# Making a scatter wait for the previous unit's scatter of the same tile, and no longer for TensorE's products

## The reference

```
x  = L0_attn_x                       # 16 x 512 tokens, 256 features, float32
xn = layernorm(x)
out = x + attention(xn) + ffn(xn)

attention: Q, K = elu(xn W + b) + 1;  V = xn Wv + bv
           KV = K^T V per sequence;  (Q KV / (Q . sum K)) Wo^T + bo     # linear attention
ffn:       scores = sigmoid(xn gate^T)                                  # 16 experts
           keep 2 of 4 groups, then the top 4 experts, weights scaled to 2.5
           sum over the 4 experts of weight * (silu(xn up_e) down_e)    # 256 -> 128 -> 256
           + silu(xn shared_up) shared_down
```

## Time and profile before

| | |
|---|---|
| timed runs, median of 3 | 972.14 us (971.48 to 979.37) |
| the profiled execution: time | 966.78 us |
| its span, first to last instruction | 964.8 us |
| mean granted clock of TensorE | 0.929 of full speed |
| TensorE, VectorE, ScalarE, GpSimd busy | 80%, 73%, 57%, 60% of the span |
| expert stage, first sum scatter to output copy | 485.8 to 929.97 us |

### The profile page before, as it was taken

The page is one execution under the profiler, slowest core; times in us unless marked ns, Lnnn a source line. Parts: engine busy times, 40 slices in busy tenths (PEclk is TensorE's granted clock), DMA queues, the critical chain, the costliest instruction groups (busy, mean ns, idle before and its releaser), DMA issues. The chain is left out here.

```text
span 964.8 us, 19765 instructions
## 1 busy us (share of the span) xinstructions
PE 768.8 (80%) x5264; PEld 704.2 (73%) x5264; DVE 700.7 (73%) x2390; ACT 553.1 (57%) x1142; POOL 581.4 (60%) x581
## 2 busy tenths in 40 slices
PE   4999999999999999997377767687676776776760
PEld 4899999999899988886266666676675775765750
DVE  5989898888888999999466555665556665656550
ACT  5677677676677766663155545554545544555440
POOL 1067766666777766666556565665555566656662
PEclk9999999999999999999599899998889888999795
DMA  5245554554445433332599888888887887888889
GB/s 156 71 171 193 186 176 179 194 187 175 149 159 188 146 129 129 114 116 112 177 288 284 239 266 266 252 261 268 245 252 250 270 267 247 265 264 261 249 277 304
DMA packets 142316, 202.15 MB, mean 210 GB/s; under 512 B 16176, under 2 KB 117184, under 8 KB 142208
## 3 DMA queue, kind: packets, MB, share of 16 engines
q1 hardware_dynamic: 114144, 116.47, 41.8%
q0 software_dynamic: 28064, 84.43, 22.8%
HBM read 104.19 MB, written 105.04 MB: 217 GB/s over the span
## 5 line engine op out<-in xcount | busy, mean ns | idle before, releaser
L574 POOL DMA_INDIRECT rows_by_expert<-xn,f_id x286 | 279.8, 978 | 194.4 <-issue 64.5
L490 POOL DMA_INDIRECT rows_by_expert<-xn,slots_now x192 | 196.9, 1026 | 122.8 <-PE bank_a L316 59.1
L1245 DVE TENSOR_TENSOR xt_l<-bank_a,xt_h 128x512 fp32r<-128x512 f32 x143 | 98.3, 687 | 97.1 <-ACT xt_h L698 67.4
L719 ACT ACTIVATE hid<-bank_x 128x256 f32<-128x256 f32 x143 | 55.3, 387 | 147.3 <-PE bank_x L316 71.5
L698 ACT CAST xt_h<-bank_a 128x512 fp32r<-128x512 f32 x143 | 83.8, 586 | 77.7 <-PE bank_a L1446 49.7
L316 PE MATMUL bank_y<-we,hs_h 128*128 x284 | 68.0, 333 | 68.4 <-DVE hs_l L1268 45.3
L316 PE MATMUL bank_a<-we,hs_h 128*128 x288 | 70.0, 337 | 61.9 <-DVE hs_l L1268 42.5
L316 PEld LDWEIGHTS bank_y<-we,hs_h 128*128 128x128 f32 x284 | 49.4, 210 | 82.3 <-issue 82.2
L316 PEld LDWEIGHTS bank_a<-we,hs_h 128*128 128x128 f32 x288 | 51.4, 216 | 75.0 <-issue 74.6
L316 PE MATMUL bank_y<-ws,hs_h 128*128 128x256 f32 x512 | 94.4, 282 | 1.4 <-DVE hs_l L997 1.4
L316 PE MATMUL bank_x<-xt_h,ws 128*128 128x512 f32 x256 | 92.1, 401 | 0.0
(11 more groups left out here) (289 smaller groups left out, 2427.7 us busy)
## 6 DMA issues: line engine op xcount, KB each, us to landing
xn<-rows_by_expert SPq DMA_DIRECT2D x215, 272.0 KB
x_in<-rows_by_expert SPq DMA_DIRECT2D x71, 272.0 KB
rows_by_expert<-spare SPq DMA_DIRECT2D x22, 544.0 KB
x_in<-in_L_attn_x_dram SPq DMA_DIRECT2D x16, 512.0 KB
out_dram<-rows_by_expert SPq DMA_DIRECT2D x8, 1024.0 KB
rows_by_expert<-xn,f_id POOLq DMA_INDIRECT x286
rows_by_expert<-xn,slots_now POOLq DMA_INDIRECT x256
w_raw<-in_L_ffn_expert_up_dram SPq DMA_DIRECT2D x32, 64.0 KB
```

Source lines behind the costliest of these rows:

```text
L490: G.indirect_dma_start(out=half_rows[:, :], in_=xn[:, c % NB, s, 0:RW], in_offset=None, out_offset=bass.IndirectOffsetOnAxis(ap=slots_now[ ...
L574: G.indirect_dma_start(out=half_rows[:, :], in_=f_y[u % YB][:, tile], in_offset=None, out_offset=bass.IndirectOffsetOnAxis(ap=f_id[:, u % ...
L719: S_.activation(f_hid[u % 2], X[u % 2][:, 0:UR], ACT.Silu).then_inc(fs_done, 1)
L1245: V.tensor_tensor(f_l[u % 4], A[u % 2][:, :].rearrange("p (c s t) -> p c s t", c=KD, s=2), f_h[u % 4].bitcast(F32), ALU.subtract).then_inc ...
```

## The change

The waits on `fd_done` and `fu_done` go. Tile 0 of unit u now waits until tile 0 of unit u - 1 has landed, and tile 1 until tile 1 of unit u - 1 has. So that such a landing can be told apart, there is a semaphore for each tile, and two classes of units in place of four: four semaphores as before, each counting 16 a unit. SP's waits follow: for each of the two classes both tiles' semaphores are waited for, with one number from the table.

```diff
-    CLS = 4
+    CLS = 2
...
-        added = [sem(f"added{i}") for i in range(CLS)]
+        added = [[sem(f"added{k}_{tile}") for tile in range(2)] for k in range(CLS)]
...
         def adds_until(u):
-            return PRIMED + 32 * (u // CLS + 1)
+            return PRIMED + 16 * (u // CLS + 1)
...
+            def landed(u):
+                for k in range(CLS):
+                    needed = four_from(mybir.EngineType.SP, 2 + k, u, PRIMED, PRIMED + 16 * UNITS)
+                    for tile in range(2):
+                        sp.wait_ge(added[k][tile], needed)
+                        sp.sem_inc(sums_free, 1)
+
             def load_sums(u):
                 if u == 4:
                     sp.wait_ge(scattered[(B - 1) % NB], scatters_until(B - 1))
                 if u >= YB:
-                    sp.wait_ge(added[(u - YB) % CLS], adds_until(u - YB))
-                for k in range(CLS):
-                    sp.wait_ge(added[k], four_from(mybir.EngineType.SP, 2 + k, u, PRIMED, PRIMED + 32 * UNITS))
-                    sp.sem_inc(sums_free, 1)
+                    for tile in range(2):
+                        sp.wait_ge(added[(u - YB) % CLS][tile], adds_until(u - YB))
+                landed(u)
...
             for u in range(UNITS):
                 pool.wait_ge(y_ready, u + 1)
                 pool.wait_ge(id_ready, u + 1)
-                pool.wait_ge(added[u % CLS], adds_until(u - CLS) if u >= CLS else PRIMED)
                 for tile in range(2):
-                    if u >= 2:
-                        if tile == 0:
-                            pool.wait_ge(fd_done, min(u + 2, UNITS))
-                        else:
-                            pool.wait_ge(fu_done, min(u + 4, UNITS))
+                    if u == 0:
+                        pool.wait_ge(added[0][tile], PRIMED)
+                        pool.wait_ge(added[1][tile], PRIMED)
+                    if u >= 1:
+                        pool.wait_ge(added[(u - 1) % CLS][tile], adds_until(u - 1))
                     G.indirect_dma_start(
                         out=half_rows[:, :], in_=f_y[u % YB][:, tile], in_offset=None,
                         out_offset=bass.IndirectOffsetOnAxis(ap=f_id[:, u % YB, tile:tile + 1], axis=0)
-                    ).then_inc(added[u % CLS], 16)
+                    ).then_inc(added[u % CLS][tile], 16)
```

More of the change, by code:

```diff
@@ L410, in _ @@
             sp.wait_ge(scattered[(B - 3) % NB], scatters_until(B - 3))
-            sp.wait_ge(scattered[(B - 2) % NB], scatters_until(B - 2) - 16 * CLS)
+            sp.wait_ge(scattered[(B - 2) % NB], scatters_until(B - 2) - 16 * SUB)
             for k in range(CLS):
-                sp.wait_ge(added[k], PRIMED)
+                for tile in range(2):
+                    sp.wait_ge(added[k][tile], PRIMED)
             row_of = {}
@@ L442, in _ @@
                     load_sums(u - (ROWS_AHEAD - SUMS_AHEAD))
-            for k in range(CLS):
-                sp.wait_ge(added[k], four_from(mybir.EngineType.SP, 2 + k, UNITS, PRIMED, PRIMED + 32 * UNITS))
-                sp.sem_inc(sums_free, 1)
+            landed(UNITS)
             out_flat = out.rearrange("b s d -> (b s) d")
@@ L452, in _ @@
             for k in range(CLS):
-                sp.wait_ge(added[k], adds_until(UNITS - 1 - (UNITS - 1 - k) % CLS))
+                for tile in range(2):
+                    sp.wait_ge(added[k][tile], adds_until(UNITS - 1 - (UNITS - 1 - k) % CLS))
             sp.wait_ge(out_stored, 16 * PARTS)
@@ L498, in scatter_first @@
                     out_offset=bass.IndirectOffsetOnAxis(ap=slots_now[:, c % NB, s, 0:1], axis=0)
-                ).then_inc(added[s] if c == B - 2 else scattered[c % NB], 16)
+                ).then_inc(added[s // 2][s % 2] if c == B - 2 else scattered[c % NB], 16)
             pool.wait_ge(consts_made, CONSTS)
@@ L1132, in plan_rows @@
                 planned()
-                plan(V.tensor_scalar(u_class_n[:, :, :], u_class_i[:, :, :], 2, None, ALU.logical_shift_right))
+                plan(V.tensor_scalar(u_class_n[:, :, :], u_class_i[:, :, :], CLS.bit_length() - 1, None,
+                                     ALU.logical_shift_right))
                 planned()
-                V.tensor_scalar(u_tab[:, :, 2:2 + CLS].rearrange("p j k -> p k j"), u_class_n[:, :, :], 32.0, float(PRIMED), ALU.mult, ALU.add
+                V.tensor_scalar(u_tab[:, :, 2:2 + CLS].rearrange("p j k -> p k j"), u_class_n[:, :, :], 16.0, float(PRIMED), ALU.mult, ALU.add
                                 ).then_inc(plan_made, 1)
```

## The result

The changed kernel takes 1098.55 us (median of 4 runs, 1093.10 to 1101.50) against 975.46 us for the kernel before on the same chip: a ratio of **1.126**, with a 95% interval from 1.118 to 1.133. It is slower by 123 us. The forecast was 1078 us, inside a range that holds the result. The execution profiled took 1098.91 us.

What follows compares the result with a forecast made beforehand. The expert stage was taken as a chain of transfers with holes, no engine full, DMA 85% busy. 134 units x (4.05 - 3.26) = +106 us on 966.78 gives 1073, with 5.4 for the median 1078 us; range 985 to 1135.

Steps and rivals of the forecast that it cites:

- Step (2): Expert stage's sum scatters: each waits for the same tile's landing one unit back, so the chain sets 4.05 us a unit.
- P: Time per unit in the expert stage: forecast 4.05 us, ends 3.4 and 4.5, against 3.26 before.
- Last packet: Time from a sum scatter's start to its last packet in the expert stage: 3.15 us forecast.
- the line: Scatter's time to its last packet rises linearly with DMA busy share: 2.1 us at nothing, 3.4 us at 0.85.
- Semaphore and restart: From a scatter's last packet to the next scatter's start on GpSimd: 0.4 us semaphore plus 0.5 us restart.
- That crowding follows the pace: In the expert stage, a slower pace leaves DMA engines less busy: 2.77 us of work a unit, busy 2.77/P.
- the first rival: Scatters land quickly with only two in flight, below 2.36 us, so the added wait stops binding: near 945 us, chance 0.10.
- Step (1): Removing GpSimd's waits on fd_done and fu_done gains at most 31 us of SP's waits, or nothing.
- Step (3): Fewer classes: SP reads fewer table lines, 0.15 us a unit less, hidden behind its semaphore waits; no gain.
- Step (4): Last eight units' scatters beside the output copy: 4.5 us each, 36 us against 34.8; adds nothing, 10 us if slower.
- far from 0.5 us: Sign that the forecast is wrong: GpSimd's restart after a landing differs much from the 0.5 us taken.

Runs made afterwards that it cites:

- the first experiment: The kernel before with both waits for TensorE taken away and nothing in their place: 1025.19 us, ratio 1.050.
- the second group: Four follow-up kernels run on another chip, the quick one, where the kernel before took 856.66 us.
- the pause: Three small GpSimd instructions behind each unit's second scatter, added to the kernel before without both waits for TensorE: 989.53 us, ratio 1.156.

## Why the prediction was right, and where not

**Step (2), the chain, held.** P was to be 4.05 us and is 4.149 (4.09 on another chip). It hardly differs whether TensorE is waited for or not (4.221 against 4.149), and is gone when the wait stands two units back. That is shown by runs that changed one thing each. That it falls by 0.08 when 0.28 are taken from tile 0's restart is weaker evidence, since two runs of the changed kernel itself differ by 0.06.

**Its terms.** Last packet: 2.84 us for tile 0 and 3.20 for tile 1, mean 3.02, where the line gave 3.15 at a DMA share of 0.68; the share came out at 0.67. Semaphore and restart together: 1.29 and 0.93 us, where I had 0.4 + 0.5 = 0.9. This was the term sized too small, by 0.2 us a unit or 28 us in all; the landing was sized too large by 0.13, which gives 17 us back. That the pace came out within 0.1 us owes something to these two errors having opposite signs. Tile 0 is slower to restart since its landing wait stands in an instruction of its own, ahead of the scatter that carries the waits for the data; put the other way round it is 1.01 us.

**That crowding follows the pace**, the idea behind the line, has the support of the run with half the rows: less traffic, earlier last packets. A line through two points was good enough at the shares of these stages (3.15 us forecast, 3.02 measured). Above 0.85 it is not: at 0.99, in the run with tile 0's wait alone, the last packet comes after 4.2 us and not 3.6. The rule in the Trainium skill (DMA: Bandwidth & Descriptors, Anatomy of one DMA), by which a scatter would take some 2.3 us whatever else runs and the landing wait would cost nothing, is not what these scatters do under load: 2.84 and 3.20 us to the last packet here, 3.4 in the kernel before, 4.2 in the run with the DMA engines 99% busy. With only two in flight the time did not fall to 2.1 us, which is what the first rival needed. On quiet engines the trace agrees with the rule: the last six scatters of the changed kernel, behind the copy, have their last packet after 2.04 to 2.11 us, within 0.3 us of its 2.3. What the Trainium skill says on the same page of the memory's longer wait under load (Latency and other measured facts) goes the way of these numbers, but no run here tells the memory's part in them.

**Step (1) was wrong.** I took the removal of the waits for TensorE at nothing, with a gain of up to 31 us as the other end. By itself it costs 50 us, shown three times over (1.050, 1.049, and 1.049 with the landing two back). SP's waits for landings, from which the gain was to come, did go away (1.7 us in the first experiment's expert stage, 31.2 before); the halts behind TensorE's late updates grew by more, as far as the traces show. The error did not reach the sum, since a chain of landings, once it binds, hides it: with the waits for TensorE the changed kernel is no faster. So the 2 us by which a scatter started later than its data was no loss to be won back, and reading it as "the difference is mostly the wait that the change removes" was right about GpSimd and wrong about the kernel. I had allowed this edit a gain or nothing and no loss, though an edit that lets work run together can cost as well.

**Step (3), nothing, held**: landing two back with the waits for TensorE is within 0.6%.

**Step (4), the tail, was too small.** I had it level with the copy and 10 us if slower; it is 12.5 us slower. From unit 135 on a unit takes 5.98 us, not 4.5: the copy's packets hold a scatter up more than the loads do, with pauses of 5 to 7 us:

```profile
1067.20 0.96 POOL L579 DMA_INDIRECT rows_by_expert<-xn,f_id  x1 [6.92 <-DMA rows_by_expert<-xn,f_id]
1068.46 0.96 POOL L579 DMA_INDIRECT rows_by_expert<-xn,f_id  x1 [0.30 <-issue]
1075.13 0.96 POOL L579 DMA_INDIRECT rows_by_expert<-xn,f_id  x1 [5.71 <-DMA rows_by_expert<-xn,f_id]
1076.39 0.96 POOL L579 DMA_INDIRECT rows_by_expert<-xn,f_id  x1 [0.30 <-issue]
```

The line gives 3.6 us to the last packet at a share of 0.98; beside the copy, at 0.91 to 0.98, it came after 5.0 to 6.8 us. The share alone thus does not set the landing, for 0.99 beside loads goes with 4.2. The trace ahead of the prediction had this already: in the kernel before, the scatters beside the copy have their last packet after 4.8 to 6.3 us. The 20 us by which the forecast fell short of 1098 are the pace (0.099 us x 134 = 13 us) and the tail (12), less 5 us by which I had set the median above the profiled execution, where it came out level.

**What the profile was to show**: GpSimd's idle time 270 us or more (339), ended by a DMA; first tiles 4 us apart; the share near 0.7 (0.67); a lower clock (0.86); never over two scatters in flight (so it is); more of SP's waits for landed sums than 31 us (289 in the stage). All came as said, but for the output copy, which came at 1049.84 us and not at 1036, by the pace. A restart "far from 0.5 us" was to prove the forecast wrong; my reckoning gives semaphore and restart together, 1.11 us in the mean against 0.9, so this sign can't be read by itself.

**What stays open** is why, on two chips, TensorE's updates come late, and with them the engines halt together. What the traces show: over 2 us late are 11 to 15% of them in the three kernels of that kind of chip that keep a wait for TensorE and have no landing wait that binds (ratios 1, 1.006 and 1.012), 32 to 35% in the three without any (1.050, 1.049, 1.049), and none in the changed kernel. So the waits for TensorE go with shorter lateness and with shorter rows of scatters; that they cause it by holding GpSimd back is my reading, since no run varied the lateness by itself. What is ruled out as the sole cause: the row of scatters itself, which on the second group's chip is 220 long and harmless; and the landing, which does not bind. Whether the kernel without both waits would be as harmless on that chip was not tried: the pause made that run another case.

## What to carry to other kernels

A wait on the landing of the transfer just before turns a queue into a chain: its pace is time to the last packet plus semaphore plus restart, here 4.1 us for two scatters where GpSimd could do 2.5, on each of the three chips. Estimate the landing at the crowding that the new pace will have, take a whole microsecond for semaphore and restart, and look separately at places where a large copy runs beside the chain. And a wait that seems to hold work back for nothing may pace it: before counting its removal as a gain, take it away alone and look.

## What was not expected of the hardware

The kernel before took 974, 857 and 965 us (medians) on the three chips of the experiments. On the quick one, in the run without tile 1's wait, the pace of the expert stage was GpSimd's (2.56 us a unit), with the DMA engines 99% busy at 330 GB/s and a granted clock of 0.99; in the trace ahead of the prediction it is 3.26 us, 0.85 and 260 GB/s, and 0.90. What makes the chips differ no run here tells. One difference shows in the traces: TensorE's semaphore updates come over 0.5 us late in 150 of 284 cases in the kernel before on one chip, and in none of the four kernels profiled on the quick one (the kernel before is not among them). Whether that is what makes the slower chips slow is not shown. The comparison of a change is thus one for each kind of chip: the change costs 13% on the slower kind and about 24% on the quick one, where the run had the tail relaxed.

From a scatter's last packet to the start of the scatter that waits for it never less than about 0.6 us passed in the changed kernel, in the middle 0.7 to 1.2, longer where the wait is an instruction of its own.
